# A fused two-layer adapter kernel: A_down gathered once a block of tokens, one transposition a chunk, GpSimd's chunk loop written out

## What is computed

```python
def lora_add(base, inp, A, B):            # A, B: the adapter of each item
    t = jnp.einsum('bri,bni->bnr', A[0][lora_indices], inp)
    return base + jnp.einsum('bor,bnr->bno', B[0][lora_indices], t) * SCALE
gate = lora_add(jnp.einsum('bnh,fh->bnf', x, W_gate), x, A_gate, B_gate)
up   = lora_add(jnp.einsum('bnh,fh->bnf', x, W_up), x, A_up, B_up)
act  = jax.nn.silu(gate) * up
down = lora_add(jnp.einsum('bnf,hf->bnh', act, W_down), act, A_down, B_down)
```

## Time and profile before

| | |
|---|---|
| median of 3 runs | 723.53 us (723.34 to 724.62) |
| the profiled execution | 725.0 us |
| its span, first to last instruction | 723.1 us |
| granted clock of TensorE, mean | 0.991 |
| chunk stage | about 180 to 640 us |
| gathers into `ab` | 88, of 128 rows of 1536 B |
| moved by DMA | 88.90 MB, of it 27.27 MB on GpSimd's queue |

### The profile page before, as it was taken

How to read it: one execution, slowest core, us unless ns; L and a number is a source line. 1 busy time by engine, 2 the same in 40 slices (tenths; PEclk the granted TensorE clock), 3 DMA queues, 4 the chain that set the end, 5 groups by cost and what they waited for, 6 DMA issues and landing times.

```text
span 723.1 us, 11495 instructions
## 1 busy us (share of the span) xinstructions
PE 689.0 (95%) x3432; PEld 574.2 (79%) x3432; DVE 350.6 (48%) x716; ACT 286.0 (40%) x605; POOL 317.4 (44%) x266
## 2 busy tenths in 40 slices
PE   4799999997999999999999989999999999979997
PEld 3588888886788888888888868888888888867775
DVE  3788676644622442642343672344263244334564
ACT  2775542213543333543333564333354333333210
POOL 0133400301777665486665387666548666300000
PEclk9999999998999999999999999999999999998999
DMA  8974451301244336244434225433424533100113
GB/s 297 362 263 159 164 203 59 103 0 45 80 154 142 112 103 227 90 128 146 123 109 139 88 90 155 127 112 107 146 88 133 152 113 112 51 2 0 59 63 112
DMA packets 30801, 88.90 MB, mean 123 GB/s; under 512 B 4609, under 2 KB 4737, under 8 KB 29217
## 3 DMA queue, kind: packets, MB, share of 16 engines
q1 hardware_dynamic: 21936, 61.05, 25.5%
q0 software_dynamic: 8672, 27.27, 12.0%
q10 hardware_dynamic: 144, 0.00, 0.0%
HBM read 78.35 MB, written 9.96 MB: 122 GB/s over the span
## 4 chain that ended last, share of the span: by engine, by line
PE 84%; DVE 4%; DMA 3%; issue 3%; ACT 2%; DVEq 1%; POOL 1%; ACTq 0%; SPq 0%; POOLq 0%
PE psD L1332 10%; PE psD L1333 10%; PE psD L1334 9%; PE psG L1332 6%; PE psG L1334 5%; PE psG L1333 5%; PE psU L1333 5%; PE psU L1334 5%; PE psU L1332 5%; PE psX L1332 2%; PE psX L1333 2%; PE psX L1334 2%; PE psD L1402 2%; PE psD L1403 1%; PE psD L1404 1%
## 5 line engine op out<-in xcount | busy, mean ns | idle before, releaser
L554 POOL TENSOR_TENSOR gu_lo<-gu_raw,gu_hi 128x1024 fp32r<-128x1024 f32 x44 | 107.8, 2451 | 130.9 <-ACT gu_hi L639 130.7
L853 DVE TENSOR_TENSOR bu<-ab,bu 64x512 fp32r<-64x512 f32 x44 | 74.8, 1699 | 74.5 <-ACT bu L639 74.3
L589 POOL DMA_INDIRECT ab<-in_ab,idx_row x88 | 87.0, 989 | 47.8 <-POOL idx_row L583 34.3
L1228 DVE TENSOR_TENSOR act_f<-psU,silu 128x512 f32<-128x512 f32 x44 | 30.4, 691 | 139.8 <-ACT silu L796 139.8
L796 ACT ACTIVATE silu<-psG 128x512 f32<-128x512 f32 x44 | 26.2, 596 | 148.3 <-PE psG L1339 143.2
L554 POOL TENSOR_TENSOR dn_lo<-dn_raw,dn_hi 128x512 fp32r<-128x512 f32 x44 | 67.4, 1533 | 30.6 <-ACT dn_hi L639 29.9
L1332 PE MATMUL psG<-x_hi,gu_hi 128*128 128x512 f32 x176 | 72.8, 414 | 0.2
L1332 PE MATMUL psD<-act_hi,dn_hi 128*128 128x512 f32 x176 | 69.0, 392 | 0.0
L1333 PE MATMUL psD<-act_lo,dn_hi 128*128 128x512 f32 x176 | 69.0, 392 | 0.0
L1333 PE MATMUL psG<-x_lo,gu_hi 128*128 128x512 f32 x176 | 68.9, 392 | 0.0
L1334 PE MATMUL psG<-x_hi,gu_lo 128*128 128x512 f32 x176 | 68.9, 392 | 0.0
(11 more groups left out here) (323 smaller groups left out, 1594.1 us busy)
## 6 DMA issues: line engine op xcount, KB each, us to landing
gu_raw<-in_gu SPq DMA_DIRECT2D x44, 512.0 KB, 3.5
dn_raw<-in_dn SPq DMA_DIRECT2D x44, 256.0 KB
cond_w_raw<-in_cond_w SPq DMA_DIRECT2D x8, 1024.0 KB, 8.1
x_all<-in_x_t SPq DMA_DIRECT2D x4, 1024.0 KB, 11.2
tok<-h_scratch SPq DMA_DIRECT2D x4, 1024.0 KB, 5.6
out_t<-x_all SPq DMA_DIRECT2D x16, 256.0 KB, 2.2
ab<-in_ab,idx_row POOLq DMA_INDIRECT x88, 3.2
kraw<-in_kern SPq DMA_DIRECT2D x1, 1024.0 KB, 14.2
```

Of the source, the lines that this page charges most:

```text
L554: pool.tensor_tensor(dst, x, hi, ALU.subtract).then_inc(s, 1)
L589: pool.indirect_dma_start(ab[:, par, g, :], None, a["ab"], bass.IndirectOffsetOnAxis(idx_row[:, par, g:g + 1], 0)).then_inc(S[f"ab_in{par} ...
L853: dve.tensor_tensor(dst, x, hi, ALU.subtract).then_inc(s, 1)
L1228: dve.tensor_tensor(act_f[:], psU[:], silu[:], ALU.mult).then_inc(S["act_f_s"], 1)
```

## The change

A_down is gathered separately. A view `a_rows` takes the same table as rows of 128 numbers, of which every third is A_down; `idx_down` holds three times the index, on the first 64 partitions that of group 0 and on the last 64 that of group 1. One more gather a chunk brings 128 rows of 512 B into `ad_raw`, and one transposition of it gives both groups side by side, 128 columns. ScalarE copies these 128 columns to the high places of `ad`, and VectorE writes the low places from the same 128. The gathers into `ab` still bring A_down along, unread. TensorE waits in addition for the new gather (`ad_in0`, `ad_in1`). GpSimd's loop over the chunks becomes straight code, which makes the chunk number a constant: the indices are read from the tables directly, and the copy to `idx_row` with its wait goes. VectorE makes `idx_down` with two operations behind `idx_fix`, which they wait for, and the waits of SP and GpSimd for `idx_tab_ready` go from 2 to 4.

```diff
--- before.py
+++ after.py
@@ -188,7 +188,6 @@
         rb_raw = sb("rb_raw", [P, D], F32)
         idx_tab = sb("idx_tab", [P, GROUPS, NF], U32)
         idx_fix = sb("idx_fix", [P, GROUPS, 2], U32)
-        idx_row = sb("idx_row", [P, 2, NGT], U32)
 
         tri = sb("tri", [P, NBIN, N_ADP], F32, at=s1_at)
         pre = sb("pre", [P, 2, NBIN, N_ADP], F32, at=s1_at + 4 * NBIN * N_ADP)
@@ -340,6 +339,8 @@
         dn_raw = sb("dn_raw", [P, D], F32)
         dn_hi, dn_lo = pair("dn", [P, 2, D])
         ab = sb("ab", [P, 2, NGT, STAB], F32)
+        ad_raw = sb("ad_raw", [P, 2, P], F32)
+        idx_down = sb("idx_down", [P, NTB, NF], U32)
         bu = sb("bu", [P, 2, NGT, 2 * P], F32R)
         ad = sb("ad", [P, 2, NGT * P], F32R)
         tm_at = top["at"]
@@ -373,6 +374,7 @@
 
         h0_dram = nc.dram_tensor("h0_scratch", [TOKENS + SLOTS * ITEM_T, D], F32, kind="Internal").ap()
         fix_rows = a["fix"].rearrange("n (k d) -> (n k) d", k=3)
+        a_rows = a["ab"].rearrange("n (k d) -> (n k) d", k=3)
 
         names = """ids0_in const_in shared_in gate_in small_in ids1_in lora_a_in lora_b_in kraw_in late_in
             w_in0 w_in1 w_in2 w_in3 w_in4 w_in5 w_in6 w_in7
@@ -384,7 +386,7 @@
             wf_hi_s wf_lo_s
             h0_in0 h0_in1 h0t_ps h0t_hi h0t_lo ae_s be_s ae_l be_l t0_ps t0_m t0_hi t0_lo x1_ps x1_f x1_hi_s x1_lo_s
             fix_in at_ps at_hi_s at_lo_s tg_ps tg_m tg_hi_s tg_lo_s bd_hi_s bd_lo_s
-            idx_r gu_in dn_in ab_in0 ab_in1 gu_hi_s gu_lo_s bu_hi_s bu_lo_s dn_hi_s dn_lo_s
+            gu_in dn_in ab_in0 ab_in1 ad_in0 ad_in1 gu_hi_s gu_lo_s bu_hi_s bu_lo_s dn_hi_s dn_lo_s
             ad_ps ad_hi_s ad_lo_s gate_ps up_ps silu_s act_f_s act_hi_s act_lo_s td_ps dn_ps
             td_m td_hi_s td_lo_s h_ps h_out0 h_out1 h_hi_s h_lo_s r_ps r_sb sc_ps sc_v exp_s soft_v mexp_s mask_ps
             xa_m xa_hi xa_lo lin_ps out_ps out_v out_st""".split()
@@ -514,7 +516,7 @@
             def load_second():
 
                 sp.wait_ge(S["x1_f"], C * NTB)
-                sp.wait_ge(S["idx_tab_ready"], 2)
+                sp.wait_ge(S["idx_tab_ready"], 4)
                 sp.wait_ge(S["mask1_ready"], 1)
                 sp.dma_start(wf_raw[:], a["wf"]).then_inc(S["late_in"], 16)
                 sp.dma_start(ra_raw[:], a["ra"]).then_inc(S["late_in"], 16)
@@ -565,7 +567,7 @@
                 scatter(b)
 
             multiplied(pool)
-            pool.wait_ge(S["idx_tab_ready"], 2)
+            pool.wait_ge(S["idx_tab_ready"], 4)
 
             def fixed(t):
 
@@ -578,54 +580,48 @@
                                                 bass.IndirectOffsetOnAxis(idx_fix[:, NGT * t + g, k:k + 1], 0)
                                                 ).then_inc(S["fix_in"], 16)
 
-            def rows(t, fc, par, n):
-
-                pool.tensor_copy(idx_row[:, par, :].unsqueeze(2), idx_tab[:, NGT * t:NGT * t + NGT, bass.ds(fc, 1)]
-                                 ).then_inc(S["idx_r"], 1)
-                count = value(pool, n + 1)
-                alone(pool)
-                pool.wait_ge(S["idx_r"], count)
+            def rows(t, fc):
+
+                par = fc % 2
                 for g in range(NGT):
                     pool.indirect_dma_start(ab[:, par, g, :], None, a["ab"],
-                                            bass.IndirectOffsetOnAxis(idx_row[:, par, g:g + 1], 0)
+                                            bass.IndirectOffsetOnAxis(idx_tab[:, NGT * t + g, fc:fc + 1], 0)
                                             ).then_inc(S[f"ab_in{par}"], 16)
+                pool.indirect_dma_start(ad_raw[:, par, :], None, a_rows,
+                                        bass.IndirectOffsetOnAxis(idx_down[:, t, fc:fc + 1], 0)
+                                        ).then_inc(S[f"ad_in{par}"], 16)
 
             def low_gu(par, n):
                 pool.wait_ge(S["gu_hi_s"], n + 1)
                 low(gu_lo[:, par, :], gu_raw[:], gu_hi[:, par, :], S["gu_lo_s"])
 
-            def gathered(par, n):
+            def gathered(n):
 
                 pool.wait_ge(S["bu_hi_s"], n)
                 pool.wait_ge(S["bu_lo_s"], n)
                 pool.wait_ge(S["ad_ps"], n)
 
             def open_block(t):
-                gathered(0, NF * t)
-                rows(t, 0, 0, NF * t)
-                rows(t, 1, 1, NF * t + 1)
+                gathered(NF * t)
+                rows(t, 0)
+                rows(t, 1)
                 low_gu(0, NF * t)
 
             def body(t):
-                def step(fc, j, par):
-                    n = NF * t + fc
+                for fc in range(NF):
+                    n, par = NF * t + fc, fc % 2
                     if not last(fc):
                         low_gu(1 - par, n + 1)
                     pool.wait_ge(S["dn_hi_s"], n + 1)
                     low(dn_lo[:, par, :], dn_raw[:], dn_hi[:, par, :], S["dn_lo_s"])
                     if not last(fc) and not last(fc, 1):
-
-                        used = value(pool, n + 1)
-                        alone(pool)
-                        gathered(par, used)
-                        rows(t, fc + 2, par, n + 2)
-                    if isinstance(fc, int) and fc == 0:
+                        gathered(n + 1)
+                        rows(t, fc + 2)
+                    if fc == 0:
                         pool.wait_ge(S["bd_hi_s"], t + 1)
                         low(bd_lo[:], fix_b[:], bd_hi[:], S["bd_lo_s"])
                     if last(fc, 1) and t < NTB - 1:
                         fixed(t + 1)
-
-                chunks(pool, step, 1, 2)
 
             fixed(0)
             for t in range(NTB):
@@ -784,7 +780,8 @@
                         high_bu(1 - par, (NF // 2 + par) * t + j + par + 1)
                     act.wait_ge(S["ad_ps"], n + 1)
                     act.wait_ge(S["dn_ps"], n if first else n - 1)
-                    high(ad[:, par, :], psX[:, 0:NGT * P], S["ad_hi_s"])
+                    high(ad[:, par, :].rearrange("p (g k n) -> p g k n", g=NGT, k=2)[:, :, 0, :],
+                         psX[:, 0:P].rearrange("p (g n) -> p g n", g=NGT), S["ad_hi_s"])
                     act.wait_ge(S["dn_in"], 16 * (n + 1))
                     high(dn_hi[:, par, :], dn_raw[:], S["dn_hi_s"])
                     if last(fc, 1) and t < NTB - 1:
@@ -1022,6 +1019,11 @@
                 dve.scalar_tensor_tensor(out=idx_fix[:], in0=idx_base[:].unsqueeze(2).broadcast_to([P, GROUPS, 2]),
                                          scalar=3.0, in1=cst("fix_row").unsqueeze(1).broadcast_to([P, GROUPS, 2]),
                                          op0=ALU.mult, op1=ALU.add).then_inc(S["idx_tab_ready"], 1)
+                dve.wait_ge(S["idx_tab_ready"], 2)
+                by_pair = idx_tab[:].rearrange("p (t g) f -> p t g f", g=NGT)
+                for g, r in enumerate((slice(0, HALF), slice(HALF, P))):
+                    dve.tensor_scalar(idx_down[r], by_pair[r, :, g, :], 3.0, None, ALU.mult
+                                      ).then_inc(S["idx_tab_ready"], 1)
 
             def scatter_rows():
 
@@ -1215,8 +1217,8 @@
                     if not last(fc):
                         low_bu(1 - par, n + 1)
                     dve.wait_ge(S["ad_hi_s"], n + 1)
-                    lower_ad = ad[:, par, :].rearrange("p (g k n) -> p g k n", g=NGT, k=2)[:, :, 1, :]
-                    low(lower_ad, psX[:, 0:NGT * P].rearrange("p (g k n) -> p g k n", g=NGT, k=2)[:, :, 1, :], lower_ad,
+                    parts = ad[:, par, :].rearrange("p (g k n) -> p g k n", g=NGT, k=2)
+                    low(parts[:, :, 1, :], psX[:, 0:P].rearrange("p (g n) -> p g n", g=NGT), parts[:, :, 0, :],
                         S["ad_lo_s"])
                     if last(fc, 1) and t < NTB - 1:
                         taken.extend(block_cols(dve, t + 1))
@@ -1541,9 +1543,8 @@
                         if first:
                             pe.wait_ge(S["tg_m"], 4 * (t + 1))
                         pe.wait_ge(S["ad_lo_s"], n)
-                        for g in range(NGT):
-                            mm = pe.transpose(psX[:, g * P:g * P + P], ab[:, par, g, 0:P], ident)
-                        mm.then_inc(S["ad_ps"], 1)
+                        pe.wait_ge(S[f"ad_in{par}"], 16 * ((NF // 2 + 1 - par) * t + j + 1))
+                        pe.transpose(psX[:, 0:P], ad_raw[:, par, :], ident).then_inc(S["ad_ps"], 1)
 
                     def gate_or_up(k, ps):
                         for c in range(C):
```

## The result

| | before | after |
|---|---|---|
| median | 724.08 us (723.34 to 726.23, 4 runs) | 739.52 us (739.37 to 739.80, 4 runs) |
| span of the profiled execution | 723.1 us | 737.4 us |
| granted clock, mean | 0.991 | 0.988 |

The changed kernel is slower: ratio 1.0204, 95% interval [1.0189, 1.022]. 718.8 us was predicted, with a range of 717.2 to 721.9; the prediction was wrong, in its sign too. Two later comparisons gave the same, 738.73 and 740.17 us.

A forecast was written before the change was run, and what follows sets the result against it. TensorE was taken as the bound, gapless in steady chunks. Terms 3.9 + 0.3 (first chunks' transpositions) + 0.9 - 0.4 = 4.7 us saved, from a median of 723.53 to 718.8 us, range 717.2 to 721.9.

The forecast's parts named there:

- GpSimd loses the index copy and its wait: Steady chunk on GpSimd: without them both ab gathers issue about 0.8 us earlier; GpSimd is free 0.5 us later.
- What hides this is its idle time of 2.63 us in front of gu_lo: Steady chunk: GpSimd's idle time absorbs its being free 0.5 us later with three gathers, so no cost.
- The size of one transposition, 0.109 us: TensorE, each chunk: dropping one of two transpositions saves 0.109 us, bounds zero and 0.22.
- the 3.9 of the sum: Gapless chunks, third onward in each block: 36 transpositions saved at 0.109 us each, 3.9 us gained.
- Rival (b): Second transposition costs nothing, as change-over price or because waits take as long: 723.0 us, chance 0.08.
- Block 0, +0.9: Third chunk's wait: bu_lo gets its turn when bd_lo ends, 0.9 us gained, ends -0.8 and +1.1.
- the three cases that were priced: Block 0, bu_lo's turn: after bd_lo, 1.0 us wait gone; one turn later, gain 0.4; after dn_lo, loss 0.8.
- Blocks 1 and 3, "at zero": Block starts where the transposition pair is on time: no change, ends -0.3 and 0 us.
- Block 2, -0.4: Longest block-start wait: bd_lo ends 0.4 us later and VectorE's low parts with it, ends -1.5 and +1.5.
- (c): Rival: GpSimd becomes the bound through straight code and a third gather; 735.7 us if 2.5 us longer; chance 0.04.
- (a): Rival: block starts turn out badly, 1.6 us gained, 721.9 us, usually about 721; chance 0.20.

The follow-up runs named there:

- f2: Changed kernel with 64 bytes of room behind idx_fix, its later tiles 32 bytes above their places in the kernel before: 729.20 us, ratio 1.0053.
- f4: Changed kernel at its own addresses with a second transposition of the same ad_raw a chunk: 733.03 us, ratio 1.0099.
- h3: Changed kernel with idx_row's 32 bytes kept and bd_lo in two halves at chunks 4 and 5, run again: 724.07 us, ratio 0.9995.
- h2: Changed kernel with idx_row's 32 bytes kept, run again beside the unpadded changed kernel: 731.09 us, ratio 1.0092.
- h4: Kernel before, unchanged, run again for its trace on the same chip as the changed kernel: 725.13 us, ratio 1.0008.
- g2: Changed kernel with idx_row's 32 bytes kept and bd_lo moved from chunk 0 into two halves at chunks 4 and 5: 725.88 us, ratio 1.0012.
- g3: Kernel before with GpSimd's loop written out, two transpositions kept, bd_lo in two halves at chunks 4 and 5: 725.63 us, ratio 1.0022.

## Why the prediction was wrong

Two terms are missing from the sum, and together they outweigh everything in it.

**"GpSimd loses the index copy and its wait".** This is the step that failed first. Where the prediction goes through the other engines it counts for `idx_row` the copy and the wait, and never the tile's 32 bytes; the spacing of TensorE's products is taken as unchanged. The removal puts the operands of 36 products a chunk at unequal remainders: +9.1 us in the changed kernel. No row of before could have given its price; the allocation order in the code shows the shift, though.

**"What hides this is its idle time of 2.63 us in front of gu_lo".** Right for the steady chunk (2.1 us of idle time left, as worked out). The ends of blocks have no term in the sum. There the same gathers form an unbroken run of six, and in comparisons of one kind TensorE's updates that fall due in it come 2 to 5 us late: +10.1 us (721.03 to 731.09, one program on two chips), of which the traces show 9.7. The prediction asked what waits for the gathers and not what happens beside them. That the gathers' place sets this off is shown by the two kernels that moved them, and by the kernel before, whose four gathers of `fixed` do the same where nobody waits; how they hold an update back is not shown. The changed kernel itself never met a comparison with complete records; some 730 us is my estimate for it there (740.17 less 10.1; its neighbour f2 took 729.20).

With -4.1 for the rest (721.03 for 725.14) this makes +15.1; measured side by side, 740.17 less 724.87, is +15.3.

**The size of one transposition, 0.109 us.** The mechanism was right, and so was the size of the transposition itself; what a chunk gains with it was sized too small. With the room kept the period is 9.73 us (9.71 and 9.74 in turn): 0.155 less than 9.88, of which the transposition is 0.11 (378.14 to 378.25 in f4, the kernel with a second one, below). The 256-column products are spaced 118 ns for 120, twelve of them 0.02 us, and the twelve of `down` 228 ns for 229, as much again; why they are closer is not known. 36 x 0.155 is 5.6 us for the 3.9 of the sum. Rival (b), a second transposition for nothing, is out. The Trainium skill (TensorE: Matmul & The Clock Gate, "Back-to-back issue gap") has about 81 ns for a sustained matmul of 128 columns; the row has 0.11 us, and the row decides.

```profile
378.14 0.27 PE L1547 MATMUL psX<-const,ad_raw 128*128 128x128 f32 x1
378.25 0.27 PE L1548 MATMUL psX<-const,ad_raw 128*128 128x128 f32 x1
```

**Block 0, +0.9.** Wrong sign. The chain was right and the turn was not. Version with the room kept, in front of the third chunk:

```profile
191.26 0.94 POOL L591 DMA_INDIRECT ad_raw<-in_ab,idx_down  x1 [0.31 <-issue]
192.22 2.42 POOL L557 TENSOR_TENSOR bd_lo<-fix_b,bd_hi 128x1024 fp32r<-128x1024 f32 x1
...
194.25 4.52 DVE L851 TENSOR_TENSOR bu<-ab,bu 64x512 fp32r<-64x512 f32 x1 [4.49 <-ACT bu L636]
...
194.58 2.39 POOL L557 TENSOR_TENSOR gu_lo<-gu_raw,gu_hi 128x1024 fp32r<-128x1024 f32 x1
...
196.93 1.28 POOL L557 TENSOR_TENSOR dn_lo<-dn_raw,dn_hi 128x512 fp32r<-128x512 f32 x1
...
199.23 0.32 PE L1548 MATMUL psX<-const,ad_raw 128*128 128x128 f32 x1 [1.37 <-DVE ad L851]
```

bd_lo ends at 194.6, as forecast, with bu_lo waiting since 194.25. It did not get its turn there nor at the end of gu_lo, and ended 0.6 us behind dn_lo, the worst of the three cases that were priced (the earlier trace rows had 3.81 us). It was ready later, too: the gathers were 0.8 us earlier, as forecast, but bu_hi only 0.25 (193.59), so bu_lo came at 194.25 and not at 193.7. The wait is 1.37 us for 0.84. The Trainium skill (SBUF — State Buffer, "SBUF: two separate sides") says that the loser of the shared port is blocked for the whole instruction; the trace agrees: bu_lo, 0.69 us where nothing meets it, stands still through the rest of bd_lo, gu_lo and dn_lo and takes 4.52 us.

**Blocks 1 and 3, "at zero".** Wrong for the same reason: 10.73 us between the second and third transposition for 10.21. bd_lo, pushed back by the third gather, is followed at once by gu_lo, and bu_lo takes 4.07 us. With bd_lo out of the way it takes 0.69 us; timeline of h3, start of block 1:

```profile
309.32 2.40 POOL L557 TENSOR_TENSOR gu_lo<-gu_raw,gu_hi 128x1024 fp32r<-128x1024 f32 x1
...
311.75 0.69 DVE L852 TENSOR_TENSOR bu<-ab,bu 64x512 fp32r<-64x512 f32 x1 [3.68 <-ACT bu L637]
```

On one chip, moving bd_lo took 11.38 to 9.83, 10.68 to 10.15, 13.56 to 12.92 and again 10.68 to 10.15 us between the second and third transposition of the four blocks, and the whole from 731.09 to 724.07 us (h2 and h3).

**Block 2, -0.4.** 13.59 for 13.06 us, so about right. The chunk behind it takes 9.8 to 10.1 us in some traces and 11.2 or more in others, of the kernel before as well (9.96 in its first trace, 11.56 in the later one, h4). The difference is TensorE's clock: in the longer ones it was granted at half right behind the wait of 2.5 to 3.3 us in front of this block's third transposition, in h4

```profile
433.30:436.70 3.40, 3.40 (x10) 2.63 (x9) 0.69 (x1) 1.50 (x2) 2.95 (x3) 0.50 0.52 161
```

where the same chunk of the first trace has 1.00. 14 of the 20 traces have this stretch, with and without the change; the prediction has no term for the clock.

**Rivals.** (c) named the right side, 735.7 us, for a reason that is not there: gu_lo still waits for gu_hi, and straight code with two transpositions was 2.4 us faster than before. (a), badly turned block starts, came true in part and would have left a gain.

## What to carry to other kernels

Removing or resizing a small tile moves all that is allocated behind it: compare the addresses of TensorE's operands before and after, and keep the room, or align, before judging a change by its time. Work given to an engine with idle time is free only where the idle time is: look at the fullest stretch (here a block's start and end), and at what else is in flight there. And if a step's place is free, as bd_lo's was, move it out of the crowd: that alone took the ratio from 1.0092 to 0.9995 on one chip. Of these 7.0 us the traces put 3.3 at the starts of blocks, where the forecast of g2 had 3 to 4; 1.4 lie in a less late update, and 1.6 in a half-clock stretch that the one trace has and the other has not, so that they are not surely its own. And a wait of TensorE can cost more than its length, when the clock is at half behind it.

## What was not expected of the hardware

- 512-column fp32r products of up are spaced 227 ns when both operands lie at the same remainder modulo 64 bytes and 233 to 234 ns when they do not (averages of steady chunks); for those of `down` it is 228 to 230 and 232 to 235.
- The comparisons fall into two kinds. In three of them every trace holds all semaphore updates (6938 to 6944 for the changed kernel with room added or a second transposition); in three, and in the changed kernel's first trace, about a quarter is missing (5149 to 5335 for the changed kernel and its versions; for the kernel before 5379 of 6274, a seventh; 5437 in g3). In the second kind TensorE's updates came up to 4.85 us behind their product, for 0.29, when they fell due in four or six gathers without a pause, in the kernel before too (up to 2.5 us). Every execution was recorded by the profiler; whether updates come late without it, no run here tells.
- Between VectorE and GpSimd a waiting subtraction can lose its turn twice in a row: bu_lo took 0.69, 4.07 and 4.52 us for the same work.
- Behind waits of 2 to 3 us in the chunk stage TensorE's clock was at times granted at half (0.50, 1.2 GHz) for 3.4 us, and 512-column products were 0.43 us apart for 0.23.
